# Graph attention, one core: x transposed in six jobs of 512 tokens, reciprocals and their DMAs moved by half a slot

## The reference

```python
q = _heads(seq_inputs @ Wq + bq)
k = _heads(seq_inputs @ Wk + bk)
v = _heads(seq_inputs @ Wv + bv)
scores = jnp.einsum('bhqd,bhkd->bhqk', q, k) / np.sqrt(HEAD_SIZE)
bias = jnp.where(graph_mask, 0.0, NEG)[:, None]
probs = jax.nn.softmax(scores + bias, axis=-1)
ctx = jnp.einsum('bhqk,bhkd->bhqd', probs, v)
...
return ctx @ Wf + bf
...
x = _layernorm(x + _L0_gnn_ref(x, ..., adj), axis=-1)
```

## Time and profile before

| | |
|---|---|
| median of 3 runs | 1580.09 us (1570.0 to 1587.43) |
| profiled execution: its own time | 1580.77 us |
| its span | 1578.5 us |
| TensorE busy | 1484.5 us (94%) |
| VectorE, ScalarE busy | 880.2 us, 878.3 us (56% each) |
| GpSimd busy | 376.7 us (24%) |
| mean granted TensorE clock | 0.994 |

### The profile page before, as it was taken

How to read it: one execution, slowest core, us unless ns; L and a number is a source line. 1 busy time by engine, 2 the same in 40 slices (tenths; PEclk the granted TensorE clock), 3 DMA queues, 4 the chain that set the end, 5 groups by cost and what they waited for, 6 DMA issues and landing times.

```text
span 1578.5 us, 31676 instructions
## 1 busy us (share of the span) xinstructions
PE 1484.5 (94%) x11088; PEld 1142.6 (72%) x11088; DVE 880.2 (56%) x1688; ACT 878.3 (56%) x1653; POOL 376.7 (24%) x676
## 2 busy tenths in 40 slices
PE   7999899999999999999999999999999999999995
PEld 6777677776877767776777776877677776777664
DVE  5566545655456655555555564555545565455553
ACT  4666535666366653666536665366644666446562
POOL 0222232121322213222133221332212322123222
PEclk9999999999999999999999999999999999999998
DMA  3021110211002111121101221012110021001111
GB/s 123 15 58 29 24 30 15 58 28 28 26 18 55 28 28 26 18 58 28 25 26 18 58 28 28 26 17 56 28 28 26 18 68 28 14 24 18 28 21 27
DMA packets 95540, 51.41 MB, mean 33 GB/s; under 512 B 56704, under 2 KB 95360, under 8 KB 95360
## 3 DMA queue, kind: packets, MB, share of 16 engines
q1 hardware_dynamic: 95360, 49.12, 13.1%
HBM read 36.31 MB, written 12.78 MB: 31 GB/s over the span
## 4 chain that ended last, share of the span: by engine, by line
PE 64%; DMA 14%; issue 9%; ACT 6%; DVE 4%; SPq 3%; DVEq 1%; POOL 0%; ACTq 0%; POOLq 0%
PE score_ps L434 15%; PE turn_ps L447 13%; PE context_ps L460 13%; DMA spread_dram<-inv_sum 12%; ACT prob L548 4%; PE misc_ps L347 4%; PE misc_ps L349 4%; PE misc_ps L348 4%; PE score_ps L347 2%; PE score_ps L349 2%; PE score_ps L348 2%; PE misc_ps L355 1%; SPq L305 1%; DMA inv_rows<-spread_dram 1%; DVE prob L651 1%
## 5 line engine op out<-in xcount | busy, mean ns | idle before, releaser
L548 ACT ACTIVATE prob<-prob,row_min 128x1024 f32<-128x1024 f32 x384 | 440.0, 1146 | 506.4 <-DVE row_min L651 489.5
L651 DVE CUSTOM_DVE_ANT_0 prob<-score_ps,mask 128x1024 f32<-128x1024 f32 x384 | 454.9, 1222 | 255.7 <-PE score_ps L434 229.8
L447 PE MATMUL turn_ps<-ident,prob 128*128 128x128 f32 x3072 | 414.4, 277 | 33.1 <-ACT prob_t L557 23.9
L447 PEld LDWEIGHTS turn_ps<-ident,prob 128*128 128x128 f32 x3072 | 337.1, 140 | 130.6 <-issue 77.5
L460 PE MATMUL context_ps<-prob_t,v_all 128*64 128x256 f32 x3072 | 372.9, 386 | 0.8 <-ACT prob_t L557 0.8
L796 POOL TENSOR_TENSOR context_lo<-context,context_hi 128x256 fp32r<-128x256 f32 x96 | 70.5, 735 | 1034.7 <-ACT context_hi L571 1034.7
L460 PEld LDWEIGHTS context_ps<-prob_t,v_all 128*64 128x64 f32 x3072 | 205.0, 137 | 145.9 <-issue 61.2
L557 ACT ACTIVATE prob_t<-turn_ps 128x512 f32<-128x512 f32 x384 | 224.5, 585 | 46.6 <-PE turn_ps L447 45.9
L660 DVE COPY prob_t<-turn_ps 128x512 f32<-128x512 f32 x192 | 132.5, 690 | 32.4 <-PE turn_ps L447 31.3
L434 PE MATMUL score_ps<-k_hi,q_hi 64*128 64x512 f32 x768 | 141.3, 446 | 5.6 <-issue 4.6
L434 PE MATMUL score_ps<-k_lo,q_hi 64*128 64x512 f32 x768 | 120.8, 391 | 0.0
(11 more groups left out here) (85 smaller groups left out, 1774.6 us busy)
## 6 DMA issues: line engine op xcount, KB each, us to landing
x_in<-in_x_dram SPq DMA_DIRECT2D x32, 384.0 KB, 5.5
inv_rows<-spread_dram SPq DMA_DIRECT2D x192, 64.0 KB, 3.9
out_dram<-res SPq DMA_DIRECT2D x32, 384.0 KB, 2.8
adj_in<-in_adj_dram SPq DMA_DIRECT2D x64, 128.0 KB, 3.4
spread_dram<-inv_sum SPq DMA_DIRECT2D x96, 2.0 KB
prob_t<-in_L_gnn_Wk_dram SPq DMA_DIRECT2D x1, 576.0 KB, 4.3
prob_t<-in_L_gnn_Wq_dram SPq DMA_DIRECT2D x1, 576.0 KB, 7.1
prob_t<-in_L_gnn_Wv_dram SPq DMA_DIRECT2D x1, 576.0 KB, 8.5
```

The costliest lines, as they stand in the source:

```text
L447: last = pe.transpose(turn_ps[:, half, i, :], prob[:, u % 4, kt * P:(kt + 1) * P], ident[:])
L548: nc.scalar.activation(prob[:, t % 4, :], prob[:, t % 4, :], ACT.Exp, scale=-1.0, bias=row_min[:, t % 4:t % 4 + 1], accum_out=row_sum[:, t ...
L651: nc.vector.tensor_tensor_reduce(prob[:, t % 4, :], score_ps[:, t % 2, :], mask[:, qt, :], 1.0, HUGE, ALU.add, ALU.min, row_min[:, t % 4:t ...
```

## The change

- The x of the next batch is transposed in six jobs of 512 tokens by 128 features (4 transposes each) instead of eight of 128 tokens by 384 features (3 each). They stand alone in slots 7, 13, 19, 20, 21, 22; nothing stands behind the second turn any more.
- K (0, 0) and Q (0, 0) of the next batch move from slots 21 and 22 to `TAIL`, which now holds all six K jobs and three Q jobs.
- V tiles 4 and 6 are made in the bank of the context (`AHEAD`), behind the scores of slots 1 and 2; tiles 5 and 7 and the later Q jobs take the places in `MID` up to slot 8. The half product of the context always stands ahead of the first turn.
- x is loaded in four pieces, in slots 3, 5, 7, 9, and the residual rows are made in slots 1 to 4 instead of 4 to 7.
- ScalarE copies the first turn's first half ahead of its first exponential, and takes the second exponential last.
- `denominators` of pair p moves on VectorE from the end of slot 2p+1 to slot 2p+2, behind its masks, and `spread` on SyncE goes with it.

```diff
+def x_jobs():
+    return [("x", t, half) for half in range(2) for t in range(3)]
...
-MID = {1: ("v", 4, 0), 2: ("v", 6, 0), 3: ("v", 7, 0), 4: ("q", 0, 1), 5: ("q", 1, 1), 7: ("q", 2, 1), 8: ("q", 0, 2),
...
-MID_NEXT = {19: ("x", 1, 0), 20: ("x", 3, 0), 21: ("k", 0, 0), 22: ("q", 0, 0)}
-END = {1: ("v", 5, 0)}
-END_NEXT = {18: ("x", 0, 0), 19: ("x", 2, 0), 20: ("x", 4, 0), 21: ("x", 5, 0), 22: ("x", 6, 0), 23: ("x", 7, 0)}
-TAIL = (("k", 0, 1), ("k", 1, 0), ("k", 1, 1), ("k", 2, 0), ("k", 2, 1), ("q", 1, 0), ("q", 2, 0))
+AHEAD = {1: ("v", 4, 0), 2: ("v", 6, 0)}
+MID = {1: ("v", 5, 0), 2: ("v", 7, 0), 3: ("q", 0, 1), 4: ("q", 1, 1), 6: ("q", 2, 1), 8: ("q", 0, 2), 9: ("p", 0, 0),
...
+MID_NEXT = dict(zip((7, 13, 19, 20, 21, 22), x_jobs()))
+TAIL = tuple([("k", pair, half) for pair in range(3) for half in range(2)] + [("q", pair, 0) for pair in range(3)])
...
# SyncE, body
                     if s % 6 >= 4 and (s // 6 < 2 or with_next):
                         load_adjacency(b, s // 6 + 1, s % 6 - 4)
-                    if s % 2 == 1:
-                        spread(b, s // 2)
-                    if s == 9 and with_next:
-                        sp.wait_ge(res_done, b * TT + TT)
-                        load_x(b + 1)
+                    if s % 2 == 0 and s:
+                        spread(b, s // 2 - 1)
+                    if s in (3, 5, 7, 9) and with_next:
+                        g = (s - 3) // 2
+                        sp.wait_ge(res_done, b * TT + (2 * g + 2))
+                        load_x(b + 1, g)
                     if s in (13, 19):
                         store(b, (s - 13) // 6)
+                spread(b, PAIRS - 1)
...
# TensorE, body
-                    scores(b, s)
-                    if mid and mixing:
+                    scores(b, s, with_next)
+                    if s in AHEAD:
+                        ahead(b, AHEAD[s], with_next)
+                    if mixing:
                         mix(b, *mixing)
                     turn(b, 2 * s - 2)
                     if mid:
                         misc(b, mid, with_next)
-                    elif mixing:
-                        mix(b, *mixing)
                     turn(b, 2 * s - 1)
-                    if end:
-                        misc(b, end, with_next)
...
# ScalarE, body
-                    exponential(b, 2 * s)
                     if s:
                         copy_first(b, 2 * s - 2)
-                    exponential(b, 2 * s + 1)
+                    exponential(b, 2 * s)
...
                         copy_odd_second(b, 2 * s - 1)
-                    if end and end[0] == "x":
-                        high_part(b, end)
+                    exponential(b, 2 * s + 1)
...
# VectorE, body
+                    if s % 2 == 0:
+                        denominators(b, s // 2 - 1)
                     if mixing and mixing[1] == 1:
                         divide(b, mixing[0])
                     copy_even_second(b, 2 * s - 2)
...
-                    if s % 2 == 1:
-                        denominators(b, s // 2)
...
                 divide(b, PAIRS - 2)
+                denominators(b, PAIRS - 1)
                 copy_even_second(b, UNITS - 2)
...
# GpSimd, body
-                    if 4 <= s < 8:
-                        residual(b, s - 4)
+                    if 1 <= s < 5:
+                        residual(b, s - 1)
```

More of the change, by code:

```diff
@@ L90, in batch_jobs @@
     for s in range(1, SLOTS):
-        jobs += [job for job in (mid_job(s, with_next), end_job(s, with_next)) if job]
+        jobs += [job for job in (AHEAD.get(s), mid_job(s, with_next)) if job]
     return jobs + (list(TAIL) if with_next else [])
@@ L115, in graph_attention @@
     first = first_jobs()
[L116 to L120, removed]
+    start_jobs = x_jobs() + first
+    loop_jobs = {w: [j for j in batch_jobs(w) if j[0] != "p"] for w in (False, True)}
+    loop_splits = {w: [j for j in loop_jobs[w] if j[0] != "v"] for w in (False, True)}
+    off_misc = TAIL + EARLY_V[:2] + EARLY_V[3:] + tuple(AHEAD.values())
+    misc_jobs = {w: [j for j in batch_jobs(w) if j not in off_misc] + [("p", 5, 0), ("p", 6, 0)] for w in (False, True)}
     x_tiles = x.rearrange("b (t p) h -> b p t h", p=P)
@@ L211, in graph_attention, with jobs_through, splits_through @@
         stored = [sem(f"stored{g}") for g in range(4)]
[L214 removed]
+        def jobs_through(b, job, with_next):
+            return b * len(loop_jobs[True]) + (len(start_jobs) + loop_jobs[with_next].index(job) + 1)
+        def splits_through(b, job, with_next):
             if b is None:
[L217 to L222, removed]
+                return start_jobs.index(job) + 1
+            return b * len(loop_splits[True]) + (len(start_jobs) + loop_splits[with_next].index(job) + 1)
         def score_bank(bank):
@@ L233, in job_bank @@
             if b is None:
-                return score_bank((first.index(job) + 3) % 4 if job in first else job[1] % 4)
+                return score_bank(start_jobs.index(job) % 4)
             if job in TAIL:
@@ L268, in _, with load_x @@
         def _(sp):
[L269 to L272, removed]
+            def load_x(b, g):
+                sp.dma_start(x_in[:, 2 * g:2 * g + 2, :], x_tiles[b, :, 2 * g:2 * g + 2, :]).then_inc(x_loaded[g], 16)
             def load_weight(w, src):
@@ L277, in _ @@
             load_weight(1, wk)
-            load_x(0)
+            for g in range(4):
+                load_x(0, g)
             load_weight(0, wq)
@@ L350, in three_products, with transpose_x, project_qk @@
                 return last
[L352 to L355, removed]
+            def transpose_x(b, t, half):
+                bank = job_bank(b, ("x", t, half))
+                for i in range(4):
+                    last = pe.transpose(bank[:, i * P:(i + 1) * P], x_in[:, 4 * half + i, t * P:(t + 1) * P], ident[:])
                 last.then_inc(job_done, 1)
-            def project_qk(b, kind, pair, piece, tokens):
+            def project_qk(b, kind, pair, piece):
                 w, width = (1, 512) if kind == "k" else (0, GQ)
                 feat = slice(pair * P, (pair + 1) * P)
-                tok = slice(tokens * width, (tokens + 1) * width)
+                tok = slice(piece * width, (piece + 1) * width)
                 three_products(job_bank(b, (kind, pair, piece))[:, 0:width], [
@@ L400, in misc, with ahead @@
                 else:
[L401 to L407, removed]
+                    pe.wait_ge(job_out, jobs_through(b, prior, with_next))
+                if job[0] == "x" and job[1] == 0:
+                    for g in (2 * job[2], 2 * job[2] + 1):
+                        pe.wait_ge(x_loaded[g], b * 16 + 32)
+                run(b, job)
+            def ahead(b, job, with_next):
+                pe.wait_ge(job_out, jobs_through(b, EARLY_V[1] if job == AHEAD[1] else AHEAD[1], with_next))
                 run(b, job)
@@ L503, in body @@
                 if with_next:
+                    tail_job(b, 3)
                     misc(b, ("p", 5, 0), with_next)
-                    for n in range(3, 7):
+                    for n in range(4, len(TAIL)):
                         tail_job(b, n)
@@ L511, in _ @@
             pe.wait_ge(ident_done, 1)
[L512 to L517, removed]
+            for n, (kind, t, half) in enumerate(x_jobs()):
+                if t == 0:
+                    for g in (2 * half, 2 * half + 1):
+                        pe.wait_ge(x_loaded[g], 16)
+                if n >= 4:
+                    pe.wait_ge(job_out, n - 3)
+                transpose_x(None, t, half)
             for k, job in enumerate(first):
                 pe.wait_ge(weights_done, 1 if job[0] == "k" else 2)
-                pe.wait_ge(job_out, TT if k < 4 else jobs_through(None, first[k - 4]))
-                project_qk(None, *job, job[2])
+                pe.wait_ge(job_out, 3 if k == 0 else max(6, k + 3))
+                project_qk(None, *job)
             pe.wait_ge(weights_done, 4)
```

110 lines of the change are left out of this document (53 added, 57 removed).

## The result

| | before | after |
|---|---|---|
| median | 1580.39 us (4 runs) | 1695.43 us (4 runs, 1691.45 to 1703.68) |
| profiled execution | 1580.77 us | 1692.38 us |
| span | 1578.5 us | 1690.4 us |
| mean granted TensorE clock | 0.994 | 0.958 |

The ratio is 1.074, with a 95% interval of 1.067 to 1.082: the change makes the kernel slower by 7.4%. The forecast was 1755 us, slower, in a range of 1670 to 1830. So the direction is as forecast and the time is inside the range, but the cost is not of the forecast size: 1695.43 - 1580.39 = 115 us, against 1755 - 1580.8 = 174.

The account below looks back on a forecast made before the run. TensorE, 94% busy, was taken to bound the kernel, with the spread's round trip hidden. Waits of +25.9 less 8.9 gave +17.0 us a batch: 1580.8 + 7 x (17.0 + 6) + 10 + 4, forecast 1755 us, range 1680 to 1830, low end widened to 1670.

Parts of the forecast that it names:

- SyncE's order: Spreads of pairs 1, 4, 7, 10 stand behind adjacency loads awaiting GpSimd's mask; slots 6, 12, 18 grow 7.6, 4.8, 4.7 us.
- The late reciprocals: Reciprocals behind the masks of even slots end 3.5 us later, making divisions late: small waits, such as +0.5 in slot 4.
- rival B: Only late reciprocals count, the spread getting out ahead of the adjacency wait: 1570 us, within 1%; chance 0.06.
- The trip: Round trip of the reciprocals, from spread issue to landed rows: 14.1 us, against two slots of 11.9 to 13.4.
- The tail: Slot 23 with tail: +2.7 us from moved jobs, and +5.2 from pair 10's late division, 16.3 us into slot 23.
- The clock: New waits idle TensorE four times a batch, lowering its granted clock: 6 us a looped batch, 4 in batch 8.
- The gain of 8.9 us a batch: Slots 18 to 22 -9.2, shorter slots 1 to 3 and 4 to 7, slot 14's wait -0.8, tail +2.7: -8.9 us.
- rival A: The trip stays hidden, so the kernel gains 71 us, to 1510 us; chance 0.05.
- The wait of `divide` in slot 14 goes: Loading x in pieces removes VectorE's division wait in slot 14: -0.8 us a looped batch, -6 in batch 8.
- ScalarE's new order costs nothing: On ScalarE, the first-turn copy comes earlier and the second exponential is wanted a whole slot later: no cost.
- batch 8's gain: In the last batch, about 9 us less, set against its new waits, leaving +10 us before clock effects.

Follow-up runs that it names:

- e1: The changed kernel with one edit: on SyncE, in even slots, the spread stands ahead of the adjacency load instead of behind it; 1584.09 us, ratio 0.993.
- e10: The changed kernel measured again, unedited, beside the kernel before on the chip of that call; 1754.44 us, ratio 1.100.
- e11: e6 with SyncE's order of the change alone put back: spread in even slots behind the adjacency load, reciprocals still early; 1736.18 us, ratio 1.089.
- e6: e5 with SyncE's loads of x in slots 3, 5, 7, 9 moved ahead of the adjacency load and the spread; 1526.83 us, ratio 0.954.
- e9: The kernel before with x loaded in four pieces ahead of the slot's spread, and residual rows in slots 1 to 4; 1582.35 us, ratio 0.990.
- e8: e6 with ScalarE's old order: first exponential, copy, second exponential, copies; ratio 0.960.
- e7: e6 with ScalarE's second exponential last in every slot, as the change has it; ratio 0.970.
- e2: The changed kernel with reciprocals and spread back at their old places, in odd slots; 1612.42 us, ratio 1.009.
- e5: e2 with ScalarE's second exponential directly behind the first in odd slots, even slots keeping the changed order; 1591.27 us, ratio 0.996.

## Why the prediction was right, and where its sizes were off

- **SyncE's order.** Right, and it is the cause: e1 takes it out of the change and the ratio falls from 1.100 (e10) to 0.993; e11 puts it alone into e6 and the ratio rises from 0.954 to 1.089. One edit takes the cause away and the other puts it in, and the slots that move in the traces are the ones named. The spread of pair 1 was to leave 11.0 us into slot 4 and left at 694.23 - 683.43 = 10.8.
- **The late reciprocals.** I had them at four small waits, 0.5 to 2.3 us, and rival B, the kernel with that cost alone, at 1570 us of 1580.8, 0.993. e1 is rival B, and measured 0.993 (its own expectation, 1540 to 1565 us, was too low). e6 is 3.9% below e1; it has early reciprocals, but also x ahead and one exponential elsewhere, so this price of the late place is not separated.
- **The trip.** This is the term that was mis-sized for the first measurement: 14.1 us from issue to landed rows, out of rows 2, 7 and 8. In the first profile of the change the landing of the spread took SyncE 8.2 us of waiting instead of 9.2, so in the fourth batch slot 6 grew by 6.7 us (13.1 less 6.43) and not by 7.6, and slot 12 by 2.7 (9.15 less 6.43) and not by 4.8; slot 18 grew by 4.8 there, but by 3.5 in the mean, 4.7 forecast. From the issue of the spread to that of the rows pass 8.1 to 13.0 us in the kernel before and 7.3 to 10.6 in the first profile of the change. The bounds of the trip, 12.2 to 17.2, were meant for this, and the range held both times. The means of the seven looped batches, in us more than the forecast's base (6.43 or 5.95 a slot; 32.7, the mean before, for slot 23 with the tail):

| | forecast | first profile | e10 |
|---|---|---|---|
| slots 6, 12, 18 | 17.1 | 13.5 | 16.6 |
| slots 4, 10, 16, 22 | 3.6 | 1.0 | 4.0 |
| slots 7, 13, 19 (clock) | 6 | 4.3 | 5.3 |
| slot 23 and tail | 7.9 | 7.9 | 8.7 |
| whole batch, with the gains, against the trace before | 23.0 | 15.0 | 22.9 |

In e10, where a landing takes as long as before, the sum holds, line by line within 1 us. That its 1754.4 us are the forecast's 1755 is in part luck: the kernel before had 1594.4 beside it, so the measured cost is 160 us, 174 forecast.

- **The tail.** The division of pair 10 was forecast 16.3 us into slot 23; in the fourth batch after it stands 13.9 us in (838.14, VectorE's timeline), by the shorter trip (11.3 us from issue at 826.88 to the division, 14.1 forecast) and a shorter slot 22, and 25.9 us go from there to the next batch, 24.6 forecast.

```profile
838.14 0.42 DVE L676 TENSOR_TENSOR context<-context_ps,inv_rows 128x256 f32<-128x256 f32 x1 [6.13 <-DMA inv_rows<-spread_dram]
```

- **The clock.** The 6 us a batch and the 4 us in batch 8 of the forecast's sum were my estimate, three drops behind four waits at 2 us each, and no run shows either term by itself. The traces show this in their place. In the fourth batch of the first profile slots 7 and 19 took 8.2 us at a granted clock of 0.71 and 0.70, behind waits of TensorE of 6.01 and 4.13 us, and slot 13, behind one of 2.50 us, took 5.95 at 1.00: two of three were long, by 2.3 us each. Over the seven looped batches slot 7 was long every time and slots 13 and 19 five times each, 4.3 us a batch for the three, and 5.3 in e10. In batch 8 slot 7 took 7.8 us in the first profile, and slots 7 and 13 took 7.7 and 7.6 in e10, where slots 13 and 19 of the first profile took 6.0. The mean granted clock fell from 0.994 to 0.958, and to 0.947 in e10. No run here takes the waits without the drops, so their split is read from slots and not shown by an experiment.
- **The gain of 8.9 us a batch.** Right, as far as the change's own traces show it: take the first four lines of the table from the whole batch, and 11.6 us less than before are left in both profiles, the forecast's 9.2, 0.7, 0.9 and 0.8 (the 2.7 more of the tail stand in the fourth line). e6, in which it is nearly alone, saves 1598.72 - 1526.83 = 71.9 us; rival A, the gain without any cost, had 71. But in e6's trace a looped batch takes 186.7 us against 193.4 in the trace before, 6.7 less, with slots 18 to 22 at 32.2 us, 30.2 forecast; the 71.9 rest in part on a kernel before that was 18 us slower beside e6 than beside the change, at a granted clock of 0.987 to 0.992, and no trace shows why.
- **The parts of the gain.** e9 shows the pieces of x at 1.0%; forecast were 7 x 0.8 + 6 us, 0.7%, of which the 6 us of batch 8 did not come in e9. The step "The wait of `divide` in slot 14 goes ... 27.9 us over 8 batches" was read from a line of the wrong waits. "ScalarE's new order costs nothing" was true but half: it gives nothing that e8 can show, and with the reciprocals early it costs 1.6% (e7). Two slips in the working changed little: 5.1 us late gives +4.7 in slot 12, not +4.8, and the parts named for batch 8's gain (0.7, 0.9 and 6) give 7.6 us, not 9. Batch 8 grew by 6.5 us in the first profile and by 13.0 in e10, 14 forecast.

What I did not foresee is the link that e2 and e5 showed: with the spread back in odd slots, the change's second piece of x falls behind it. The places of x and of the spread on SyncE depend on each other.

## What to carry to other kernels

In these kernels SyncE issues its DMAs in the order of its program, and a wait for one delayed what stood behind it: pair 1's spread went out 6.5 us after its reciprocals, behind the wait for a mask, and that order alone is the step from 0.954 (e6) to 1.089 (e11). Before a move, write down for each DMA when its own condition is met, and let none that is ready early stand behind one that is ready late. The round trip here was about as long as its cover (some 14 us by my estimate, against two slots of 12 to 13.4), and the 6.5 us of delay came out as 6.7 us more in slot 6. The slot behind that wait of TensorE then took 8.2 us at a granted clock of 0.71, instead of 5.95 at 1.00: count such a slot too. When an experiment that should give the gain back does not, look at what it has moved besides.

## What was not expected of the hardware

The same DMA of 2 KB (`spread_dram<-inv_sum`, 128x4x1) kept SyncE waiting 8.2 us in the mean in one measurement and 9.1 in another, with the same kernel, whose time was 1695 us in the one and 1754 in the other, 3.5% more, while the kernel before moved by 0.9% between them (1580 and 1594) and by 1.2% over all measurements here (1580 to 1599). Here, then, the kernel that is bound by such a latency repeated less well than the one bound by TensorE, and its ratio needs the two kernels side by side: the two intervals, 1.067 to 1.082 and 1.091 to 1.109, do not meet. Whether the chip or the moment makes the latency is open; in the trace before and in those of e1 to e11, on three chips, the spread takes 9.5 to 9.7 us in the mean from its issue to that of the rows, 8.7 in the first profile of the change alone.
